# Attention scores of a quad laid side by side, and a mix back whose stationary pieces have 128 columns

## The chip, the core and the metric

The kernel runs on one core of one Trainium2 chip. The time is device time in microseconds (us) from the start to the end of one execution; the number given for the kernel is the median of its runs. Engines are named as the profile names them: PE is TensorE (a matmul moves one operand through an array that holds a stationary operand, which PEld loads), DVE is VectorE, ACT is ScalarE, POOL is GpSimd, and SP is the queue that issues the DMAs.

## What is computed

A stack of two blocks on 32 sequences of 256 tokens with 128 channels, in float32. Block 0 is a selective-scan mixer with a gated feed-forward net. Block 1 is an attention with 16 heads of 64 and 4 memory keys a head, followed by another feed-forward net. The change lies in the attention of block 1, whose core is, cut to what matters:

```python
dots = jnp.einsum('bhid,bhjd->bhij', q, k) * QK_SCALE      # j: 4 memory keys, then the tokens
dots = jnp.einsum('hg,bgij->bhij', W_pre_th, dots)         # heads mixed before the softmax
dots = jnp.where(causal[None, None], mask_value, dots)
top = jax.lax.top_k(dots, TOPK)[0]                         # TOPK = 64
dots = jnp.where(dots < top[..., -1:], mask_value, dots)
attn = jax.nn.softmax(dots, axis=-1)
attn = jnp.einsum('hg,bgij->bhij', W_post_th, attn)        # heads mixed after it: the "mix back"
out = jnp.einsum('bhij,bhjd->bhid', attn, v)
```

## The kernel before

Block 0 runs first, for all sequences (to about 860 us). Then `attention_phase` runs block 1 as a pipeline over sequences. In each period of the pipeline one sequence goes through ranking and softmax while the next one's scores are made and the one before it goes through attention, output projection and feed-forward net. Every engine has a fixed order of work, written out by hand: a period has 128 beats, and tables such as `PE_MIX`, `ACT_MIX`, `POOL_SHARE` and `DVE_SHARE` say at which beat a step stands in its engine's stream. A step then runs when its semaphores allow it; nothing is reordered at run time.

**Tiling of the scores.** 128 partitions hold 8 queries (`QG`) of 16 heads, which is one group; a sequence has 32 groups. Group `g` sees 4 + 8(g + 1) keys, and its row of scores is as wide as that of the odd group of its pair: 20, 20, 36, 36, ... 260, 260 elements. All rows of a sequence lie in one tile, `T8` (two of them, for even and odd sequences), from element `ROW[g]` on. Before the change the rows lie in the order of the groups, except that row 31 lies ahead of row 30 (`ROW`, line 1075). `side(g)` is 1 where a row lies behind that of its pair.

**Quads.** Ranking, softmax and mix back go by quads: quad i is the groups 30-2i, 31-2i, 2i, 2i+1, so two wide rows and two narrow ones, together 560 elements in every quad.

**A quad's way.** SP sends scores through DRAM to regroup them by head and query (`stage`, `regroup`; lines 1277 to 1297; one DMA a pair, but two where `side(g)` of the pair's first group is 1). PE mixes the heads of a pair (`premix`, L1371), ACT copies it to `T8` (`t_keep`, L1575), POOL adds the causal mask (`hide`, L1898). DVE finds the 64 largest of every row with rounds of eight (`rank`, `wide`, `narrow`: L1752 to L1797 for wide rows, L1719 to L1735 for narrow ones). POOL marks and drops what is below (`drop`, L1923, L1933), ACT takes the exponentials (`exps`, L1551), DVE the reciprocal of the sums (`share_out`, L1704), and POOL scales the post-mix matrix with it (`share_posts`, L1882, tile `posts`).

**The mix back** (`mix_back`, lines 1373 to 1400). It multiplies each row of scores, as stationary operand, with its `posts`, which turns it to have keys on partitions. A row is cut into pieces of at most 128 columns: `first` takes elements 0 to 127 (L1383), `second` from 128 on for the wide rows (L1387), and groups 15 and 31 have one more piece of 4 columns (L1399). A last piece has as many columns as are left of the row: 20 to 116. A quad's mix back is 6 or 7 matmuls; the profile shows two records for each matmul in float32. Results lie in two PSUM banks (`ATB`), from which ACT copies them (`at_keep`, L1588 to L1596), only as many partitions as the row has keys. `back_mixed` is raised once, by the last matmul of a quad. Attention (`attend`, L1414 to L1418) follows when all quads of a sequence are copied.

**Other lines that the prediction names.** L221, L195, L250 feed-forward matmuls; L432, L453, L1437, L1448 projections; L1356 scores (`score`, stationary operand on 64 partitions), copied by ACT at L1567; L134 spreads a layer norm's factor for DVE's last step of the norm at L140 (tiles `nc_rs` and `x_c` for the first norm, `nd_rs` and `x_d` for the second).

Of the kernel before, what the change touches and what calls it, by code (L numbers as in the profile page):

```python
# [12 lines left out]
P = 128  # L13
# [4 lines left out]
HEADS, DH, MEM, TOPK = 16, 64, 4, 64  # L18
INNER = HEADS * DH
IC = INNER // P  # L20
KEYS = MEM + SEQ
KM = HEADS * MEM
QG = P // HEADS
GROUPS = SEQ // QG
NXB = 3
QUADS = GROUPS // 4
# [6 lines left out]
HALF = GROUPS // 2  # L33
# [9 lines left out]
def seen_by(group):  # L43

    return MEM + QG * (group + 1)
# [1012 lines left out]
def attention_phase(nc, sh, ctx, out):  # L1058
# [4 lines left out]
    sems, room = sh.room, Room(nc, ctx)  # L1063
# [8 lines left out]
    def width(g):  # L1072
        return seen_by(g | 1)

    ROW = [sum(width(k) for k in range(g)) for g in range(GROUPS + 1)]
    ROW[GROUPS - 2:GROUPS] = ROW[GROUPS - 2] + KEYS, ROW[GROUPS - 2]
    T8 = room.sbs("T8_", [P, ROW[GROUPS]], 2)

    def pair_scores(b, g):
        at = min(ROW[g], ROW[g + 1])  # L1080
        return T8[b % 2][:, at:at + min(2 * width(g), 512)]

    def scores(b, g, a=0, z=None):
        z = width(g) if z is None else z
        return T8[b % 2][:, ROW[g] + a:ROW[g] + z]

    def side_by_side(b, g):

        at, w = min(ROW[g], ROW[g ^ 1]), width(g)
        return T8[b % 2][:, at:at + 2 * w].rearrange("p (two n) -> p two n", two=2)  # L1090

    def side(g):
        return int(ROW[g] > ROW[g ^ 1])

    QUAD = [(30 - 2 * i, 31 - 2 * i, 2 * i, 2 * i + 1) for i in range(QUADS)]
    PREMIX = [list(range(HALF)), [g for i in range(QUADS) for g in (30 - 2 * i, 31 - 2 * i)]]
    PAIR_AT = {g: (blk * HALF + k) // 2 for blk in range(2) for k, g in enumerate(PREMIX[blk])}

# [13 lines left out]
    NP = 8  # L1112
    posts = room.sbs("posts", [P, P], NP)
# [35 lines left out]
    TURNED = [g for g in range(GROUPS) if g not in WHOLE and g not in WIDE]  # L1149
    DROPS = [[j0 for j0 in (0, 2) if QUAD[i][j0 + 1] not in WHOLE] for i in range(QUADS)]  # L1150
    DROPS_ALL = sum(len(c) for c in DROPS)
# [7 lines left out]
    def rank_steps(i):  # L1159

        n = sum(17 for g in QUAD[i] if g in WIDE) + (QUAD[i][2] not in WIDE) + 2 * len(CUT[i])
        for g in QUAD[i]:
            if g in TURNED:
# [163 lines left out]
    def tensor(pe):  # L1327
# [45 lines left out]
        def mix_back(b, i):  # L1373

            n = GROUPS * b + 4 * i
            at0, at1 = ATB
            pe.wait_ge(posts_made, n + 4)
            if n:
                pe.wait_ge(at_kept, AT_KEEPS * b + KEPT[i])

            def first(j):
                m = min(width(QUAD[i][j]), P)
                return pe.matmul(at0[0:m, j * P:(j + 1) * P], scores(b, QUAD[i][j], 0, m), posts[(n + j) % NP][:], start=True, stop=True)  # L1383

            def second(j):
                m = min(width(QUAD[i][j]), 2 * P) - P
                return pe.matmul(at1[0:m, j * P:(j + 1) * P], scores(b, QUAD[i][j], P, P + m), posts[(n + j) % NP][:], start=True, stop=True)  # L1387

            order = [(first, 0), (first, 1)]
            if width(QUAD[i][2]) <= P // 2:  # L1390
                order += [(second, 0), (second, 1), (first, 2), (first, 3)]
            else:
                order += [(first, 2), (first, 3), (second, 0), (second, 1)]
            for one, j in order:
                last = one(j)
            for j in (1, 3):
                if QUAD[i][j] in (HALF - 1, GROUPS - 1):
                    c = P if QUAD[i][j] == HALF - 1 else 2 * P
                    last = pe.matmul(at1[0:MEM, 2 * P:3 * P], scores(b, QUAD[i][j], c, c + MEM), posts[(n + j) % NP][:], start=True, stop=True)  # L1399
            last.then_inc(back_mixed, 4)  # L1400

        def attend(b, c2):
# [48 lines left out]
        for p in range(-1, PERIODS):  # L1451
            for t in range(BEATS):
# [15 lines left out]
                for i in range(QUADS):  # L1468
                    if (b := whose(p, t, PE_MIX[i])) is not None:
                        mix_back(b, i)  # L1470
# [393 lines left out]
    def gpsimd(pool):  # L1864
        for s in sh.mixed_end:
            pool.wait_ge(s, 1)
        for b in range(2):
            pool.wait_ge(sh.mid_out[b], 16 * (SEQS // 2))
        pool.memset(T8[0][:], 0.0).then_inc(zeroed, 1)
        pool.memset(T8[1][:], 0.0)  # L1870
        pool.memset(V2[:], 0.0)
# [111 lines left out]
def program(nc, d, out):  # L1983

    with ExitStack() as ctx:
        sh = Shared(nc, ctx, d)
        with ExitStack() as inner:
            mixer_phase(nc, sh, inner)
        with ExitStack() as inner:
            attention_phase(nc, sh, inner, out)  # L1990
# [63 lines left out]
```

## Time and profile before

| | |
|---|---|
| time, median of 3 runs | 3660.3 us (3659.46 to 3661.69) |
| span of the profiled execution | 3658.1 us |
| busy, share of the span | PE 94%, DVE 93%, ACT 84%, PEld 70%, POOL 48% |
| chain that ended last | PE 64%, DVE 16%, ACT 14%, issue 3%, POOL 2%, DMA 1% |
| DMA | 210.76 MB, 58 GB/s on average |

The span is the time from the first to the last instruction of one execution. Busy shares are means over the whole span, of which the first 860 us are block 0, without any of the work that changes. The views below therefore look at stretches of block 1. In the timeline a line is a group of like instructions in a row: when the first began, how long from there to the end of the last, and in brackets the idle time of the engine before it with what ended that time. PE's matmuls overlap at their ends, so the pitch of two groups (start to start) says what a group costs, and its length is some 0.2 us more.

### The profile page before, as it was taken

How to read it: one execution, taken by the hardware profiler on the slowest of the kernel's cores; microseconds unless marked ns; L12 is line 12 of the kernel's file. 1: busy time of each engine (PE TensorE's matmuls, PEld its weight loads, DVE VectorE, ACT ScalarE, POOL GpSimd, SP SyncE). 2: the span in 40 equal slices, each digit the busy share in tenths (PEclk: the TensorE clock that was granted, in tenths of full speed). 3: DMA queues.
4: the chain of work that ended last, by engine and by line, in shares of the span. 5: the costliest groups of instructions: out<-in, count | busy, mean ns of one | idle time of the engine just before them, and what ended most of it. 6: DMA issues, size and time to landing. Idle time of an engine off the chain costs nothing.

```text
span 3658.1 us, 79012 instructions
## 1 busy us (share of the span) xinstructions
PE 3438.4 (94%) x19551; PEld 2576.4 (70%) x19551; DVE 3392.9 (93%) x18541; ACT 3074.4 (84%) x10773; POOL 1743.1 (48%) x3672
## 2 busy tenths in 40 slices
PE   5999999996899999999999999999999999999997
PEld 4888888883566666666666666666666666666665
DVE  7898888854999999999999999999999999999994
ACT  6777777856799899899999899989988899989963
POOL 0000000003666666666666566666666666666653
PEclk7999999997899999999999999999999999999998
DMA  3000000002222222222222222222222222222220
GB/s 131 13 12 12 13 12 10 11 7 73 63 74 70 70 74 78 80 71 65 65 65 66 65 65 69 73 71 74 70 75 84 65 65 65 65 66 65 64 62 4
DMA packets 254141, 210.76 MB, mean 58 GB/s; under 512 B 78000, under 2 KB 234736, under 8 KB 252912
## 3 DMA queue, kind: packets, MB, share of 16 engines
q1 hardware_dynamic: 253680, 205.70, 18.0%
q8 instruction: 156, 2.56, 0.3%
q14 instruction: 305, 2.50, 0.2%
HBM read 93.97 MB, written 111.67 MB: 56 GB/s over the span
## 4 chain that ended last, share of the span: by engine, by line
PE 64%; DVE 16%; ACT 14%; issue 3%; POOL 2%; DMA 1%; SPq 0%; DVEq 0%; ACTq 0%; POOLq 0%
PE bank L363 11%; PE bank L221 7%; DVE W L1775 5%; PE bank L1383 5%; PE bank L1371 5%; PE bank L1356 4%; DVE last L1797 3%; PE bank L331 3%; PE bank L1414 3%; PE bank L453 3%; ACT SN L1567 3%; PE bank L195 3%; PE bank L1448 3%; PE bank L1428 2%; PE bank L1387 2%
## 5 line engine op out<-in xcount | busy, mean ns | idle before, releaser
L1775 DVE MATCH_REPLACE8 W<-last,W 128x130 f32<-128x130 f32 (+18 forms) x3456 | 871.0, 259 | 0.0
L1797 DVE MAX8 last<-W 128x8 f32<-128x130 f32 (+18 forms) x3456 | 761.9, 261 | 0.0
L1882 POOL TENSOR_SCALAR posts<-post,share 128x128 f32<-128x128 f32 x1024 | 366.5, 379 | 287.2 <-DVE share L1704 278.1
L894 DVE TENSOR_TENSOR_SCAN hs<-dA,dx 128x256 f32<-128x256 f32 x512 | 348.1, 680 | 86.6 <-issue 80.2
L1551 ACT ACTIVATE T<-T,peak 128x260 f32<-128x260 f32 (+15 forms) x1024 | 410.9, 409 | 4.2 <-POOL T L1933 3.3
L1567 ACT ACTIVATE SN<-bank,rq 128x260 f32<-128x260 f32 (+1 forms) x1024 | 357.8, 424 | 61.3 <-PE bank L1356 60.1
L1371 PE MATMUL bank<-T,pre 128*128 128x40 f32 (+15 forms) x1024 | 364.8, 439 | 15.0 <-ACT T L1575 10.1
L1383 PE MATMUL bank<-posts,T 128*128 128x128 f32 (+7 forms) x2048 | 310.2, 288 | 71.5 <-POOL posts L1882 63.4
L1933 POOL TENSOR_TENSOR T<-T,below 128x520 f32<-128x520 f32 (+12 forms) x416 | 360.5, 883 | 20.1 <-DVE below L1806 4.8
L1383 PEld LDWEIGHTS bank<-posts,T 128*128 128x128 f32 (+7 forms) x2048 | 247.2, 173 | 168.6 <-POOL posts L1882 93.8
L1898 POOL TENSOR_TENSOR T<-T,w_mask 128x32 f32<-128x32 f32 x512 | 141.0, 278 | 403.5 <-ACT T L1575 401.1
L1356 PE MATMUL bank<-kT,qT 64*128 64x260 f32 (+1 forms) x2048 | 274.8, 372 | 42.8 <-ACT SN L1567 33.5
L522 POOL TENSOR_SCALAR k_sq<-k_sq 128x16 f32<-128x16 f32 x64 | 17.7, 276 | 591.9 <-DVE k_sq L535 542.3
L1923 POOL TENSOR_SCALAR below<-T,last 128x244 f32<-128x244 f32 (+3 forms) x256 | 270.2, 1055 | 33.9 <-DVE last L1795 10.6
L1371 PEld LDWEIGHTS bank<-T,pre 128*128 128x128 f32 x1024 | 168.0, 191 | 164.1 <-issue 82.8
L1775 DVE MATCH_VALUE_LOAD W<-last,W 128x8 f32 x3456 | 261.0, 76 | 0.0
L221 PE MATMUL bank<-f_b,w_f1h 128*128 128x256 f32 x1024 | 248.9, 387 | 5.7 <-ACT f_b L233 5.7
L1575 ACT ACTIVATE T<-bank 128x40 f32<-128x40 f32 (+15 forms) x512 | 208.0, 406 | 51.3 <-PE bank L1371 49.2
L1520 ACT ACT_TABLE_LOAD x192 | 246.3, 1283 | 4.5 <-POOLq L1049 1.1
L221 PE MATMUL bank<-f_a,w_f1h 128*128 128x256 f32 x1024 | 248.0, 385 | 0.0
L1356 PEld LDWEIGHTS bank<-kT,qT 64*128 64x128 f32 x2048 | 146.9, 191 | 136.1 <-ACT SN L1567 74.3
L363 PE MATMUL bank<-f_b,w_f0h 128*128 128x256 f32 x1024 | 236.5, 379 | 0.0
(244 smaller groups left out, 9584.0 us busy)
## 6 DMA issues: line engine op xcount, KB each, us to landing
scores_by_token<-SN SPq DMA_DIRECT2D x64, 520.0 KB, 2.6
scores_by_token<-SN SPq DMA_DIRECT2D x64, 396.0 KB, 3.2
scores_by_token<-SN SPq DMA_DIRECT2D x32, 780.0 KB, 3.3
scores_by_token<-SN SPq DMA_DIRECT2D x32, 264.0 KB, 2.6
scores_by_token<-SN SPq DMA_DIRECT2D x32, 260.0 KB, 2.0
T<-scores_by_token SPq DMA_DIRECT2D x32, 244.0 KB, 3.1
T<-scores_by_token SPq DMA_DIRECT2D x32, 228.0 KB, 3.3
T<-scores_by_token SPq DMA_DIRECT2D x32, 212.0 KB, 3.9
```

Of the source, the lines that this page charges most:

```text
L221: last = pe.matmul(o[:, (m % 2) * SEQ:(m % 2 + 1) * SEQ], self.w[layer][:, c, m * P:(m + 1) * P], src[:, c, :], start=c == 0, stop=c == HC ...
L363: last = pe.matmul(o[:, (m % 2) * SEQ:(m % 2 + 1) * SEQ], self.w[layer][:, c, m * P:(m + 1) * P], src[:, c, :], start=c == 0, stop=c == HC ...
L894: dve.tensor_tensor_scan(hs[j % NH][:], dA[j % ND][:], dx[b % 2][:], 0.0, ALU.mult, ALU.add).then_inc(scanned, 1)
L1356: last = pe.matmul(FRONT[(n + half) % 3][:, j * w:(j + 1) * w], qT[rows, even // 2, blk * P:(blk + 1) * P], kT[rows, even // 2, 0:w], star ...
L1371: pe.matmul(MIX[:, 0:pair.shape[-1]], pre[:], pair, start=True, stop=True).then_inc(premixed, 1)
L1383: return pe.matmul(at0[0:m, j * P:(j + 1) * P], scores(b, QUAD[i][j], 0, m), posts[(n + j) % NP][:], start=True, stop=True)
L1551: act.activation(one, one, ACT.Exp, bias=peak[k % 2][:, j:j + 1], accum_out=total[k % 4][:, j:j + 1]).then_inc(e_made, 1)
L1567: last = act.activation(SN[:, h, 0:w], FRONT[n % 3][:, j * w:(j + 1) * w], ACT.Copy, scale=rq[:, c:c + 1])
L1775: dve.match_replace(both[:, s, at:to], best[n], both[:, s, at:to], LOWEST).then_inc(ranked, 1)
L1797: dve.max(best[n], both[:, s, at:to]).then_inc(ranked, 1)
L1882: pool.tensor_scalar(posts[(4 * k + j) % NP][:], post[:], share[k % 2][:, j:j + 1], 1.0, ALU.mult, ALU.mult).then_inc(posts_made, 1)
L1933: pool.tensor_tensor(x, x, out, ALU.add).then_inc(dropped, 1)
```

## The change

Two things. First, the rows of a quad lie together in `T8`: `LAID` is the order of the groups, and `ROW` follows from it. In the quads with groups 0 to 5 the narrow rows come first and then the wide ones, in the others the wide ones come first; row 31 still lies ahead of row 30, and now row 15 lies ahead of row 14 too, so `side(14)` is 1 and the pair (14, 15) is fetched by two DMAs. `T8` is as large as before (4480 elements). Second, a piece of the mix back no longer ends with its row: `tall` takes 128 columns from the piece's start wherever the quad's 560 elements reach that far, and so reads on into the next rows of the same quad. What comes of it lands in PSUM partitions that `at_keep` doesn't read. Columns of the pieces, before and after, from the two layouts:

| quad | first, four rows, before | after | second, two rows, before | after | extra piece, before | after |
|---|---|---|---|---|---|---|
| 0 | 128 128 20 20 | 128 128 128 128 | 128 128 | 128 128 | 4 | 128 |
| 1 | 128 128 36 36 | 128 128 128 128 | 116 116 | 128 116 | | |
| 2 | 128 128 52 52 | 128 128 128 128 | 100 100 | 128 100 | | |
| 3 | 128 128 68 68 | 128 128 128 68 | 84 84 | 128 128 | | |
| 4 | 128 128 84 84 | 128 128 128 84 | 68 68 | 128 128 | | |
| 5 | 128 128 100 100 | 128 128 128 100 | 52 52 | 128 128 | | |
| 6 | 128 128 116 116 | 128 128 128 116 | 36 36 | 128 128 | | |
| 7 | 128 128 128 128 | 128 128 128 128 | 20 20 | 128 128 | 4 | 128 |

The order of a quad's matmuls is now the same for all quads; before, quads 0 to 2 had the narrow rows last. The beat tables are unchanged.

```diff
@@ -1072,9 +1072,15 @@
     def width(g):
         return seen_by(g | 1)
 
-    ROW = [sum(width(k) for k in range(g)) for g in range(GROUPS + 1)]
-    ROW[GROUPS - 2:GROUPS] = ROW[GROUPS - 2] + KEYS, ROW[GROUPS - 2]
-    T8 = room.sbs("T8_", [P, ROW[GROUPS]], 2)
+    QUAD = [(30 - 2 * i, 31 - 2 * i, 2 * i, 2 * i + 1) for i in range(QUADS)]
+    LAID = [(0, 1, 31, 30)] + [(*q[2:], *q[:2]) if q[2] < HALF // 2 - 2 else q for q in QUAD[1:-1]] + [(16, 17, 15, 14)]
+    LAID = [g for four in LAID for g in four]
+    ROW = [sum(width(k) for k in LAID[:LAID.index(g)]) for g in range(GROUPS)]
+    T8 = room.sbs("T8_", [P, sum(width(g) for g in range(GROUPS))], 2)
+
+    def quad_end(i):
+
+        return max(ROW[g] + width(g) for g in QUAD[i])
 
     def pair_scores(b, g):
         at = min(ROW[g], ROW[g + 1])
@@ -1092,7 +1098,6 @@
     def side(g):
         return int(ROW[g] > ROW[g ^ 1])
 
-    QUAD = [(30 - 2 * i, 31 - 2 * i, 2 * i, 2 * i + 1) for i in range(QUADS)]
     PREMIX = [list(range(HALF)), [g for i in range(QUADS) for g in (30 - 2 * i, 31 - 2 * i)]]
     PAIR_AT = {g: (blk * HALF + k) // 2 for blk in range(2) for k, g in enumerate(PREMIX[blk])}
 
@@ -1378,25 +1383,25 @@
             if n:
                 pe.wait_ge(at_kept, AT_KEEPS * b + KEPT[i])
 
+            def tall(j, c):
+                m = min(quad_end(i) - ROW[QUAD[i][j]] - c, P)
+                return scores(b, QUAD[i][j], c, c + m), m
+
             def first(j):
-                m = min(width(QUAD[i][j]), P)
-                return pe.matmul(at0[0:m, j * P:(j + 1) * P], scores(b, QUAD[i][j], 0, m), posts[(n + j) % NP][:], start=True, stop=True)
+                x, m = tall(j, 0)
+                return pe.matmul(at0[0:m, j * P:(j + 1) * P], x, posts[(n + j) % NP][:], start=True, stop=True)
 
             def second(j):
-                m = min(width(QUAD[i][j]), 2 * P) - P
-                return pe.matmul(at1[0:m, j * P:(j + 1) * P], scores(b, QUAD[i][j], P, P + m), posts[(n + j) % NP][:], start=True, stop=True)
-
-            order = [(first, 0), (first, 1)]
-            if width(QUAD[i][2]) <= P // 2:
-                order += [(second, 0), (second, 1), (first, 2), (first, 3)]
-            else:
-                order += [(first, 2), (first, 3), (second, 0), (second, 1)]
-            for one, j in order:
+                x, m = tall(j, P)
+                return pe.matmul(at1[0:m, j * P:(j + 1) * P], x, posts[(n + j) % NP][:], start=True, stop=True)
+
+            for one, j in ((first, 0), (first, 1), (first, 2), (first, 3), (second, 0), (second, 1)):
                 last = one(j)
             for j in (1, 3):
                 if QUAD[i][j] in (HALF - 1, GROUPS - 1):
                     c = P if QUAD[i][j] == HALF - 1 else 2 * P
-                    last = pe.matmul(at1[0:MEM, 2 * P:3 * P], scores(b, QUAD[i][j], c, c + MEM), posts[(n + j) % NP][:], start=True, stop=True)
+                    x, m = tall(j, c)
+                    last = pe.matmul(at1[0:m, 2 * P:3 * P], x, posts[(n + j) % NP][:], start=True, stop=True)
             last.then_inc(back_mixed, 4)
 
         def attend(b, c2):
```

## Rows read from the trace of the kernel before

**Rows 1.** the page: span, and busy time of each engine

```profile
span 3658.1 us, 79012 instructions
...
PE 3438.4 (94%) x19551; PEld 2576.4 (70%) x19551; DVE 3392.9 (93%) x18541; ACT 3074.4 (84%) x10773; POOL 1743.1 (48%) x3672
```

**Rows 2.** stretches: busy (x) of PE, PEld, DVE, ACT, POOL; PEclk, DMA, GB/s

```profile
2396.50:2399.90 3.40, 3.39 (x13) 2.73 (x14) 3.40 (x32) 2.23 (x8) 1.99 (x6) 0.51 0.52 210
1800.00:1884.76 84.76, 81.36 (x502) 58.36 (x500) 84.11 (x533) 76.84 (x301) 53.62 (x115) 1.00 0.23 70
```

**Rows 3.** waits of DVE, 1000 to 3500 us: total, times, longest

```profile
DVE W L1752 <- POOL T L1898: 10.3, 29, 0.4
...
DVE x_d L140 <- PE bank L134: 3.2, 3, 1.1
...
DVE share L1704 <- ACT T L1551: 1.1, 3, 0.4
...
DVE x_c L140 <- PE bank L134: 0.6, 1, 0.6
```

**Rows 4.** timeline, DVE and POOL at the start of quad 0's ranking

```profile
1810.98 0.47 DVE L1795 MAX8 last<-W 128x8 f32<-128x124 f32 x2
...
1811.62 0.25 POOL L1898 TENSOR_TENSOR T<-T,w_mask 128x32 f32<-128x32 f32 x1
...
1811.91 0.43 DVE L1752 TENSOR_TENSOR W<-T 128x260 f32<-128x260 f32 x1 [0.36 <-POOL T L1898]
```

**Rows 5.** timeline, PE: mix backs of quads 3 and 1, with what follows

```profile
1800.46 1.04 PE L1383 MATMUL bank<-posts,T 128*128 128x128 f32 x8
1801.34 0.60 PE L1387 MATMUL bank<-posts,T 128*84 128x128 f32 x4
1801.78 0.56 PE L1371 MATMUL bank<-T,pre 128*128 128x232 f32 x2
...
1861.18 1.89 PE L221 MATMUL bank<-f_a,w_f1h 128*128 128x256 f32 x8
1862.91 1.03 PE L221 MATMUL bank<-f_b,w_f1h 128*128 128x256 f32 x4
...
1865.82 0.71 PE L1383 MATMUL bank<-posts,T 128*128 128x128 f32 x4
1866.37 0.60 PE L1387 MATMUL bank<-posts,T 128*116 128x128 f32 x4
1866.90 0.63 PE L1383 MATMUL bank<-posts,T 128*36 128x128 f32 x4
1867.46 1.99 PE L221 MATMUL bank<-f_b,w_f1h 128*128 128x256 f32 x8
1869.29 0.31 PE L1371 MATMUL bank<-T,pre 128*128 128x40 f32 x2
```

**Rows 6.** timeline, SP: regrouping a first half, and the next DMA

```profile
1863.42 3.94 SPq L1297 DMA_DIRECT2D T<-scores_by_token  x8
1873.71 0.34 SPq L1278 DMA_DIRECT2D scores_by_token<-SN  x1
```

**Rows 7.** timeline, PE and then DVE, where the granted clock was low

```profile
2396.51 1.20 PE L1356 MATMUL bank<-kT,qT 64*128 64x260 f32 x4 [0.65 <-ACT SN L1567]
...
2402.50 0.42 DVE L140 TENSOR_TENSOR x_d<-n_cen,bank 128x256 f32<-128x256 f32 x1 [1.08 <-PE bank L134]
```

**Rows 8.** timeline, DVE: the start of quad 0's ranking, three periods in a row

```profile
2324.29 0.43 DVE L1752 TENSOR_TENSOR W<-T 128x260 f32<-128x260 f32 x1 [0.36 <-POOL T L1898]
...
2410.22 0.43 DVE L1752 TENSOR_TENSOR W<-T 128x260 f32<-128x260 f32 x1 [0.37 <-POOL T L1898]
...
2495.38 0.43 DVE L1752 TENSOR_TENSOR W<-T 128x260 f32<-128x260 f32 x1 [0.36 <-POOL T L1898]
```

**Rows 9.** timeline, PE: the last quad of the last sequence

```profile
3610.58 1.04 PE L1387 MATMUL bank<-posts,T 128*20 128x128 f32 x4
...
3613.11 0.65 PE L1414 MATMUL bank<-AT,V 128*64 128x256 f32 x4 [1.15 <-ACT AT L1596]
```

## What the change was predicted to do

> **What bounds the kernel now.** I read the page first, then the busy time of a stretch inside block 1, then the waits of the engine that is fullest there, and last the timeline around the mix backs and around each of these waits.
>
> The page gives PE 94% and DVE 93% of the span [rows 1], and its chain names PE most often, so PE looks like the bound. The stretch of one period says otherwise: of 84.76 us DVE is busy 84.11, PE 81.36, ACT 76.84, POOL 53.62 [rows 2]. PE has 3.40 us a period in which it does nothing, DVE 0.65. Where two engines are this full, the chain runs over either of them; the question is who waits for whom. In 2500 us DVE waits 10.3 us for POOL's masks at L1752, 3.2 and 0.6 us for PE at L140, and 1.1 us for ACT's exponentials [rows 3]: 15.2 us together, 0.6%. Only 3.8 us of that, in four places, wait for PE. So block 1 is bound by DVE's rankings, and a faster PE can bring no more than what DVE waits.
>
> The 10.3 us are 29 waits of 0.36, one a period, at the start of quad 0's ranking. Does PE stand behind them? DVE's last two MAX8 of the quad before it start at 1810.98 and end at 1811.45; POOL's mask starts at 1811.62, lasts 0.25, and DVE goes on at 1811.91 [rows 4]. In POOL's stream the wait of `drop` for these MAX8 (L1916) stands ahead of that mask. It is a hand-over from DVE to POOL and back, and PE has no part in it: it keeps its 0.36 however early the premix comes.
>
> **Part 1, the switches between narrow and full pieces.** The pitch of groups (start to start) in quad 3, where no piece has 64 columns or fewer: 0.88 for eight records, 0.44 for four, 1.32 for all twelve, whether a piece has 128, 84 or 68 columns [rows 5]. Quad 1, with two rows of 36 columns: from the group of 116 columns to that of 36 it is 0.53 in place of 0.44, so 0.09 for going in. The four narrow records take 0.56 in place of 0.44, so 0.12. After them eight records of L221 take 1.83 where the same group takes 1.73 between 1861.18 and 1862.91, so 0.10 for coming out [rows 5]. Narrow pieces are not shorter (0.14 a record against 0.11), and an excursion into them costs 0.09 + 0.12 + 0.10 = 0.31 us. Quads 0, 2, 5, 6 and 7 have one excursion each as well, six a sequence with quad 1's. In quad 2 the step out stays, since what follows (L1356, on 64 partitions) is another arrangement of the array anyway: 6 x 0.31 - 0.10 = 1.76 us a sequence. The change widens all these pieces to 100 columns or more, and all of it goes.
>
> **Part 2, wider loads.** 24 matmuls of a sequence, three a quad, get wider stationary pieces: 1744 columns more by the table of the change, each loaded twice. Rows 5 show four records at 0.44 both with 84 columns and, as half of the 0.88 group, with 128 and 68; the digits would hide 0.01 at most. 24 matmuls are 12 groups of four: at most 0.12 us. I take 0.06, and 1.76 - 0.06 = 1.7 us a sequence, or 54 us of PE time over 32 sequences. A rule speaks against the change here: the Trainium skill, "TensorE: Matmul & The Clock Gate", section "LDWEIGHTS (loading the stationary operand)", says that a load takes its number of columns divided by 1.2, in ns. By it the loads grow by an estimated 1744 x 2 / 1.2 = 2.9 us a sequence, which is more than the switches give back, if they were exposed. The rows show them hidden under the matmul before, as long as the arrangement doesn't change; and even exposed they would take 1.2 us net out of PE's idle 3.4, so that the time of the kernel would be the same by either.
>
> **Where the 1.7 us go.** They don't reach DVE. PE's idle time grows from 3.40 to some 5.1 us a period, mostly ahead of the mix backs that wait for `posts` and of the score matmuls that wait for ACT's copies. ACT gets `back_mixed` earlier and waits less at L1588. Neither shortens DVE's 84.11 us, nor the hand-over.
>
> **Part 3, the order.** In quads 0 to 2 `second` now runs ahead of the narrow rows. ACT is released by the last matmul alone, so this moves nothing: 0. No wait is added: the mix back already waits for `posts` of all four rows, which come after all four exponentials, so the neighbouring rows that `tall` reads are finished.
>
> **Part 4, the new layout.** DVE, ACT and POOL do the same instructions on the same widths at other addresses, all multiples of 4 elements as before: 0. The pair (14, 15) takes two DMAs on SP. Eight of them take 3.94 us to issue, 0.49 each; SP's next DMA comes 6.4 us after the eighth is out (1873.71 against 1867.36) [rows 6]. What waits for the landing of this pair and the one before it is the premix of 232 elements, at 1801.78 in one period [rows 5] and so at 1886.5 in the next, 18.7 us after the new DMA would be issued. Hidden; without that cover it would cost 0.5 us a period, and in the first sequence, where the pipeline fills, it might show once: 0 to 0.5, I take 0.
>
> **Part 5, the end.** After the last ranking the rest is a chain of PE, ACT and POOL, and the last mix back lies on it: attention waits for ACT's copies of it [rows 9]. Going into its narrow piece falls away, 0.09 at full clock; here the record lengths are longer (1.04 for the four against 0.60 to 0.63), so perhaps 0.2. Going out stays, since attention uses 64 columns. I take -0.1.
>
> **The sum.** 3658.1 for the span, -0.1 at the end, 0 elsewhere: 3658.0. The median of the runs is 3660.3, 2.2 above the profiled span; so 3660.2 us. What a measurement of this kernel can tell from no change is about 0.2%, 7.3 us.
>
> **Rival 1, PE's clock (slower).** From 2396.50 to 2399.90 the granted clock was 0.51, the lower of the two levels, 1.2 in place of 2.4 GHz [rows 2]. Just before it PE had been waiting 0.65 us for ACT's copy, amid score matmuls and pieces of a single column. PE came late with the spread at L134, and DVE waited 1.08 us at L140 [rows 7]. From one start of quad 0's ranking to the next it took 85.93 us there and 85.16 in the next, against 84.76: 1.6 us for one such drop [rows 8]. Three waits of 3.2 us in all say that it was so in three periods of some 30 [rows 3]. The change makes PE idle more, just ahead of the scores (quads 0 and 1) and of quad 7's `posts` (quads 5 and 6). If the clock then drops in ten periods in place of three, 7 x 1.6 = 11.2 us are added: 3671. It decides from five more on (7.3 / 1.6). For it: these stretches are the emptiest already. Against it: PE also gets there earlier, which shortens the very wait at L140, and ACT moves up with it. By the Trainium skill, the same page, "Part 1: The HAM clock gate", the low clock is the default and activity releases it, so that more idling means more of it; the trace agrees in that the drop followed a stretch with waits, and whether 1.7 us more are enough no row tells.
>
> **Rival 2, PE binds after all (faster).** If DVE's waits all hang on PE in a way that the waits view puts down to others, the 15.2 us in 2500 go: 16.4 us over the 2700 of block 1, so 3644. Rows 4 speak against it, and DVE's 84.11 us of 84.76 stay.
>
> **Rival 3, the switches stay.** If the pitch hangs on something else than the number of columns, mix backs are as long as before, and the time too: 3660. Quads 3 and 4, without switches at 84 and 68 columns, speak against it.
>
> **Chances.** Forecast 0.65; rival 1 0.22; rival 2 0.06; rival 3 0.05; that the drops of the clock vanish, for -5 us, 0.02. Faster is rival 2 and a little of the unknown, 0.08; slower is rival 1, 0.22; within 0.2% is the rest, 0.70. The range goes up to rival 1's time and a little over, 3672, and down to 3654, which takes in the vanished drops and the ends of parts 2, 4 and 5. The forecast's own range is 3656 to 3664.
>
> **What the profile after would show.** Quad 1's mix back and quad 7's with all groups at 0.11 a record, and no record of L1383, L1387 or L1399 with 64 columns or fewer (part 1). PE's busy time in a period down by 1 to 2 us and its waits up by as much, at L1383 for `posts` above all. ACT's wait at L1588 smaller. DVE's 0.36 at L1752 still there, the period still 84.7 to 84.8. Nine DMA issues in the first half's regrouping, with no premix waiting for them. The count of DVE's waits at L140 decides rival 1. I am wrong if DVE's busy time or its hand-over changes, that is, if the period does.

## The result, and the profile after

The changed kernel takes 3685.2 us (median of 4 runs, 3681.9 to 3688.4), the kernel before, measured beside it, 3659.9 us (4 runs): a ratio of 1.0072, 95% interval 1.0058 to 1.0086. It is slower, by 26 us and outside the range, which ended at 3672. Lines have moved: L1383, L1387 and L1399 are now L1392, L1396 and L1404, L1356 is L1361, L1371 is L1376, L1575 is L1580, L1752 and L1755 are L1757 and L1760, L1882 is L1887, L1898 is L1903, L1925 and L1933 are L1930 and L1938.

The page first (as [rows 1]) and one undisturbed period, from one start of quad 0's ranking to the next (as the second of [rows 2]):

```profile
span 3684.6 us, 79044 instructions
...
PE 3421.0 (93%) x19551; PEld 2603.2 (71%) x19551; DVE 3416.4 (93%) x18541; ACT 3073.3 (83%) x10773; POOL 1753.3 (48%) x3672
```

```profile
1394.52:1480.02 85.50, 80.47 (x503) 58.82 (x502) 84.88 (x533) 76.76 (x300) 54.27 (x114) 1.00 0.22 69
```

PE's time went down and DVE's went up, with the same 533 instructions: 84.88 us against 84.11. The period is 85.50 in place of 84.76. And what DVE waits for has hardly changed (as [rows 3]; waits of DVE, 1000 to 3500 us):

```profile
DVE W L1757 <- POOL T L1903: 9.9, 29, 0.4
DVE x_c L140 <- PE bank L134: 3.7, 6, 0.6
DVE share L1709 <- ACT T L1556: 0.4, 2, 0.2
```

So the time sits inside DVE's instructions, where no view of waits looks. I compared a period of each kernel instruction by instruction. Two are longer in 21 of the 30 periods, all undisturbed ones among them: the first two steps (maximum and minimum of a row's halves, two inputs) for the pair (14, 15) at the start of quad 7's ranking. The timeline there, DVE and POOL, first before and then after:

```profile
1458.28 0.25 POOL L1898 TENSOR_TENSOR T<-T,w_mask 128x32 f32<-128x32 f32 x1 [0.96 <-ACT T L1575]
...
1458.63 1.47 POOL L1925 TENSOR_SCALAR below<-neg,last 128x116 f32<-128x116 f32 x2
...
1459.76 0.27 DVE L1752 TENSOR_TENSOR W<-T 128x132 f32<-128x132 f32 x1
1459.95 0.28 DVE L1755 TENSOR_TENSOR W<-T 128x132 f32<-128x132 f32 x1
...
1460.18 1.51 POOL L1933 TENSOR_TENSOR T<-T,below 128x328 f32<-128x328 f32 x2
```

```profile
1464.12 1.50 POOL L1930 TENSOR_SCALAR below<-neg,last 128x116 f32<-128x116 f32 x2
...
1465.71 1.57 POOL L1938 TENSOR_TENSOR T<-T,below 128x328 f32<-128x328 f32 x2
...
1466.06 0.69 DVE L1757 TENSOR_TENSOR W<-T 128x132 f32<-128x132 f32 x1
1466.66 0.77 DVE L1760 TENSOR_TENSOR W<-T 128x132 f32<-128x132 f32 x1
```

POOL's two additions (328 and 232 elements; they drop what `drop` has marked in quad 6) used to start 0.42 us behind DVE's first step, and now start 0.35 us ahead of it. Then each step of DVE ends 0.16 us after the addition beside it: the additions run 1465.71 to 1466.58 and 1466.55 to 1467.27, the steps end at 1466.74 and 1467.43, 0.69 and 0.77 us long in place of 0.27 and 0.28. From the first step to what follows both it is 1.29 us (the next instruction starts at 1467.35), where it was 0.40 (1460.16): 0.89 more. DVE arrives 0.12 earlier, since a marking of its own just ahead, no longer beside POOL's mask, takes 0.54 in place of 0.62. The period as a whole is 0.74 longer, x30 = 22 us.

In five other periods, each with a fall of PE's clock (a short stretch at the lower granted clock, of which more below), POOL's first addition starts 0.03 us behind DVE's first step. That step keeps its 0.27; the addition takes 0.98 in place of 0.88, and it is the second step that waits for its end:

```profile
1124.26 0.27 DVE L1757 TENSOR_TENSOR W<-T 128x132 f32<-128x132 f32 x1
1124.29 1.68 POOL L1938 TENSOR_TENSOR T<-T,below 128x328 f32<-128x328 f32 x2
1124.45 0.97 DVE L1760 TENSOR_TENSOR W<-T 128x132 f32<-128x132 f32 x1
```

Why POOL comes earlier is one row of ACT, its copy of the pair of 168 elements, first before, then after:

```profile
1457.88 0.32 ACT L1575 ACTIVATE T<-bank 128x168 f32<-128x168 f32 x1
```

```profile
1463.38 0.32 ACT L1580 ACTIVATE T<-bank 128x168 f32<-128x168 f32 x1
```

Counted from the start of quad 0's ranking (1388.10 and 1394.52) that is 69.78 and 68.86. POOL's mask of this pair had been waiting for the copy (0.96 in the rows before); its marks and additions stand behind the mask in its stream, and came along, from 72.08 to 71.19. DVE's step stayed, at 71.66 and 71.54.

The other 4 us of the profiled difference (26.5): the first start of quad 0's ranking is 2.7 later, which is scatter, since over the fourteen profiles of this case it lies anywhere from 876.4 to 882.2 us, behind code that none of them changes; 2.2 lie behind the last start of quad 0's ranking, the last collision among them; and what the 30 periods take beyond the undisturbed length (falls of the clock, mostly) sums up to 10.0 before and 9.4 after.

### The profile page after: what moved, and what is told of

Same layout as the page of the kernel before. It is cut to its first block, busy times and chain, and to the rows that moved or that the text cites. A ratio compares the mean times of both kernels' runs of the same rounds, so it can differ in the third digit from the quotient of the medians.

```text
span 3684.6 us, 79044 instructions
## 1 busy us (share of the span) xinstructions
PE 3421.0 (93%) x19551; PEld 2603.2 (71%) x19551; DVE 3416.4 (93%) x18541; ACT 3073.3 (83%) x10773; POOL 1753.3 (48%) x3672
## 4 chain that ended last, share of the span: by engine, by line
PE 53%; DVE 33%; POOL 5%; ACT 5%; issue 3%; DMA 1%; SPq 0%; DVEq 0%; ACTq 0%; POOLq 0%
PE bank L363 11%; DVE W L1780 11%; DVE last L1802 7%; PE bank L221 4%; DVE W L1732 3%; PE bank L1419 3%; PE bank L453 3%; PE bank L331 3%; PE bank L1376 3%; PE bank L1433 3%; PE bank L1453 3%; PE bank L195 2%; PE bank L1392 2%; PE bank L1361 2%; POOL posts L1887 2%
## 5 line engine op out<-in xcount | busy, mean ns | idle before, releaser
L1887 POOL TENSOR_SCALAR posts<-post,share 128x128 f32<-128x128 f32 x1024 | 366.5, 376 | 371.9 <-DVE share L1709 364.4
L1392 PEld LDWEIGHTS bank<-posts,T 128*128 128x128 f32 (+4 forms) x2048 | 258.9, 194 | 195.3 <-POOL posts L1887 170.5
L1392 PE MATMUL bank<-posts,T 128*128 128x128 f32 (+4 forms) x2048 | 297.4, 290 | 104.8 <-POOL posts L1887 102.4
L1376 PE MATMUL bank<-T,pre 128*128 128x40 f32 (+15 forms) x1024 | 365.7, 439 | 16.1 <-ACT T L1580 11.1
L1938 POOL TENSOR_TENSOR T<-T,below 128x520 f32<-128x520 f32 (+12 forms) x416 | 367.1, 898 | 20.2 <-DVE below L1811 5.0
L1361 PE MATMUL bank<-kT,qT 64*128 64x260 f32 (+1 forms) x2048 | 276.3, 374 | 42.2 <-ACT SN L1572 34.3
L522 POOL TENSOR_SCALAR k_sq<-k_sq 128x16 f32<-128x16 f32 x64 | 17.6, 275 | 595.5 <-DVE k_sq L535 542.3
L1903 POOL TENSOR_TENSOR T<-T,w_mask 128x32 f32<-128x32 f32 x512 | 143.4, 285 | 327.1 <-ACT T L1580 324.1
L1376 PEld LDWEIGHTS bank<-T,pre 128*128 128x128 f32 x1024 | 168.5, 193 | 170.2 <-issue 84.4
L221 PE MATMUL bank<-f_b,w_f1h 128*128 128x256 f32 x1024 | 245.8, 384 | 5.4 <-ACT f_b L233 5.4
L221 PE MATMUL bank<-f_a,w_f1h 128*128 128x256 f32 x1024 | 244.6, 382 | 0.0
L1361 PEld LDWEIGHTS bank<-kT,qT 64*128 64x128 f32 x2048 | 147.0, 191 | 133.9 <-ACT SN L1572 95.1
L1580 ACT ACTIVATE T<-bank 128x40 f32<-128x40 f32 (+15 forms) x512 | 206.6, 404 | 41.2 <-PE bank L1376 39.8
```

The source lines that it names most:

```text
L221: last = pe.matmul(o[:, (m % 2) * SEQ:(m % 2 + 1) * SEQ], self.w[layer][:, c, m * P:(m + 1) * P], src[:, c, :], start=c == 0, stop=c == HC ...
L1361: last = pe.matmul(FRONT[(n + half) % 3][:, j * w:(j + 1) * w], qT[rows, even // 2, blk * P:(blk + 1) * P], kT[rows, even // 2, 0:w], star ...
L1376: pe.matmul(MIX[:, 0:pair.shape[-1]], pre[:], pair, start=True, stop=True).then_inc(premixed, 1)
L1392: return pe.matmul(at0[0:m, j * P:(j + 1) * P], x, posts[(n + j) % NP][:], start=True, stop=True)
L1887: pool.tensor_scalar(posts[(4 * k + j) % NP][:], post[:], share[k % 2][:, j:j + 1], 1.0, ALU.mult, ALU.mult).then_inc(posts_made, 1)
L1938: pool.tensor_tensor(x, x, out, ALU.add).then_inc(dropped, 1)
```

## The experiments

Each ratio is to the kernel before on the same chip, with its 95% interval. The period is the median of 30, the lower of the two in the middle; an undisturbed one of before is 84.76. "Steps" are DVE's two steps of the pair (14, 15), "lead" is how far POOL's first addition starts ahead of the first step, and "falls" counts stretches from 965 to 3500 us where the granted clock fell below full. The step lengths, lead and falls are from the one profiled execution.

| kernel | ratio | period | steps | lead | falls |
|---|---|---|---|---|---|
| before | 1 | 84.79 | 0.27 0.28 | -0.42 | 4 |
| after | 1.0072 (1.0058 to 1.0086) | 85.50 | 0.69 0.77 | +0.35 | 11 |
| e1_layout_only | 1.0002 (0.9993 to 1.0012) | 84.75 | 0.27 0.28 | -0.42 | 3 |
| e2_pe_padded | 1.0077 (1.0062 to 1.0092) | 85.70 | 0.27 0.28 | -1.24 | 5 |
| e3_before_hide_late | 1.0089 (1.0073 to 1.0104) | 85.71 | see below | +1.25 | 7 |
| e4_pool_delay | 1.0030 (1.0018 to 1.0042) | 85.35 | 0.27 0.28 | -0.42 | 19 |
| e6_before_clip | 0.9983 (0.9973 to 0.9993) | 84.69 | 0.27 0.28 | -0.42 | 3 |
| e8_wide_567 | 1.0024 (1.0014 to 1.0033) | 84.76 | 0.27 0.28 | -0.33 | 13 |
| e9_wide_012 | 1.0083 (1.0068 to 1.0098) | 85.80 | 0.69 or 0.84, 0.77 | +0.35 or +0.20 | 7 |
| e10_one_input | 1.0021 (1.0012 to 1.0031) | 85.33 | 0.27 0.46 | +0.35 | 18 |
| e11_fill_567 | 1.0004 (0.9995 to 1.0014) | 84.75 | 0.27 0.28 | -0.34 | 6 |
| e12_fill_567_clip | 0.9975 (0.9964 to 0.9986) | 84.42 | 0.27 0.28 | -0.34 | 2 |
| e13_after_fill | 1.0057 (1.0040 to 1.0074) | 85.57 | 0.68 0.77 | +0.35 | 1 |
| e14_after_fill_delay | 1.0010 (1.0001 to 1.0019) | 84.99 | 0.27 0.28 | -0.42 | 11 |

The theory: POOL's additions meet DVE's steps. The rivals: the new layout or its additional DMA costs the time, or PE's clock does.

### The layout alone

The change with its new `ROW`, but the old pieces in the old order:

```diff
-            def tall(j, c):
-                m = min(quad_end(i) - ROW[QUAD[i][j]] - c, P)
...
+                m = min(width(QUAD[i][j]), P)
+                return pe.matmul(at0[0:m, j * P:(j + 1) * P], scores(b, QUAD[i][j], 0, m), ...)
```

> The new order of the rows in T8 (with two DMAs for the pair 14, 15), but the mix back cut into the same pieces and in the same order as before. Theory (the collision): PE, no longer waiting at the switches, lets ACT's copies and POOL's mask come 0.9 us earlier, so that POOL's two additions in the drop of quad 6 run at the same time as DVE's four max and min steps at the start of quad 7's ranking, and two of these take 0.69 and 0.77 us in place of 0.27 and 0.28; with the old pieces PE is slow again, the period is 84.76 us and the time 3660, within 0.2% of before. Rival (the layout): DVE reads the pair 14, 15 slower where it lies now; then the period is 85.5 and the time 3683 to 3686.

3659.5 us, 1.0002. The layout and its ninth DMA are innocent. What is left of the change is its pieces and their order in quads 0 to 2.

### PE as slow as before

After, with two matmuls into a dead place behind the mix back of every quad with an excursion:

```diff
+            if i not in (3, 4):
+                x, m = tall(1, P)
+                for n_ in (P, 48):
+                    last = pe.matmul(at1[0:m, P:P + n_], x, posts[(n + 1) % NP][:, 0:n_], start=True, stop=True)
             last.then_inc(back_mixed, 4)
```

> The changed kernel, with 128-column pieces, but in the six quads that had narrow pieces the last wide piece is multiplied once more, and once more with 48 columns moving, some 0.30 us a quad, about what a switch to narrow pieces and back took. The values are the same. Theory (the collision): only PE's time matters, so the max and min steps of the pair 14, 15 take 0.27 and 0.28 us again, the period is 84.8 and the time 3658 to 3666. Rival (the layout or the wide pieces themselves): 85.5 and 3683 to 3688.

A miss: 3686.9 us, though the collision is gone (0.27 and 0.28, POOL 1.24 late). The padding overshot: it takes 0.35 to 0.38 us in five of the six quads, up to the start of what follows, where 0.30 was meant, and the period has 82.21 us of PE's time against 81.36 before. POOL's mask is now held back to 1465.68, 71.56 behind the start of quad 0's ranking, and PE and ACT with it. DVE now waits for them (1000 to 3500 us):

```profile
DVE share L1713 <- ACT T L1560: 18.5, 29, 0.6
DVE W L1761 <- POOL T L1907: 11.2, 29, 0.5
DVE x_d L140 <- PE bank L134: 8.7, 5, 1.8
```

It doesn't speak to the collision, and it corrects me in something else: with 0.85 us more of PE's time, DVE waits for ACT's exponentials in every period, and the chain that ended last is PE 74%, ACT 16% and DVE 5%. That "block 1 is bound by DVE's rankings" was true by less than a microsecond.

### The collision in the kernel before

The kernel before, with nothing of the change: only POOL's mask of that pair moved behind `drop` of quad 6, so that nothing holds the marks and additions back.

```diff
-    POOL_PREMIX = [[92, 94, 95, 97, 112, 117, 120, 128], ...
+    POOL_PREMIX = [[92, 94, 95, 97, 116, 117, 120, 128], ...
```

> The kernel before, with one entry of POOL's order changed: the mask of the fifth pair of a sequence's first half goes behind the drop of quad 6 in place of ahead of it, so that the drop no longer waits for ACT's copy of that pair. PE, ACT and DVE have the order, pieces and layout of before. Theory (the collision): the drop's marks start 0.9 to 1.1 us earlier, its additions meet DVE's max and min steps, these take 0.4 us longer twice or more, and the time is 3678 to 3692. Rival (layout, or PE's clock): POOL's order has nothing to do with it, 3660.

3692.2 us, 1.0089, with PE and the layout untouched. DVE and POOL in its timeline:

```profile
1468.50 1.58 POOL L1933 TENSOR_TENSOR T<-T,below 128x328 f32<-128x328 f32 x2 [0.18 <-DVE below L1806]
1468.56 0.99 DVE L1755 TENSOR_TENSOR W<-T 128x148 f32<-128x148 f32 x1
...
1469.76 0.48 DVE L1752 TENSOR_TENSOR W<-T 128x132 f32<-128x132 f32 x1
...
1470.16 0.34 DVE L1755 TENSOR_TENSOR W<-T 128x132 f32<-128x132 f32 x1
```

POOL is so early here that it meets another step as well: L1755 takes 0.99 where its like takes 0.30. The three are 0.69 + 0.21 + 0.06 = 0.96 us a period longer, and the period is 85.71, 0.95 longer than an undisturbed one of before. The meeting is enough by itself to cost this much.

### The collision taken out of the changed kernel

After, with two idle POOL instructions, 0.9 us together, ahead of `drop` of quad 6:

```diff
+            if i == 6:
+                for n, w in enumerate((512, 16)):
+                    pool.wait_ge(idled, 2 * b + n + 1)
+                    pool.tensor_scalar(idle[:, 0:w], idle[:, 0:w], 1.0, 1.0, ALU.mult, ALU.mult).then_inc(idled, 1)
```

> The changed kernel, with two idle POOL instructions (0.9 us together) ahead of the drop of quad 6, on a tile that nobody reads. PE stays as fast as in the changed kernel. Theory (the collision): the additions come after DVE's max and min steps, as before, the period is 84.8, and the time 3658 to 3668; what is left over before is what PE's clock costs. Rival (the layout, or PE's clock): 3683 to 3688, or more.

3671.0 us, above the 3668 that I had expected at most: it gives 15 of the 26 us back. The steps are short again and the undisturbed period is 84.72. What is left goes with the last column of the table: 19 falls of the clock, and with them a median period of 85.35. Most of these belong to this kernel, though, and not to the changed one. Six stand 7 to 8 us behind the start of quad 0's ranking, as in the changed kernel (more on them under "Which quads do it"). Thirteen stand 71 to 72 us behind it, and there DVE waits 0.2 us for PE's spread (`x_d`) and 0.3 for ACT's exponentials, 13 times each; the changed kernel has five falls at that place, and in three of the five the period stays at 85.49.

Then POOL's additions in quad 6 as instructions of one input:

```diff
+                if i == 6:
+                    pool.tensor_scalar(x, x, 1.0, 1.0, ALU.mult, ALU.mult).then_inc(dropped, 1)
+                    continue
                 pool.tensor_tensor(x, x, out, ALU.add).then_inc(dropped, 1)
```

> The changed kernel, but POOL's two additions in the drop of quad 6 (two inputs each) are replaced by an instruction of one input on the same elements, which writes them back unchanged; so keys below the 64th stay in quad 6, and nothing else is left out. Theory (two instructions of two inputs, one on DVE and one on POOL, shut each other out): POOL works over the same stretch, yet DVE's steps at L1757 and L1760 take 0.27 and 0.28 us, and the time is 3658 to 3670. Rival (any POOL instruction at that moment slows DVE): the steps stay at 0.5 us or more, 3675 or more.

3668.2 us, DVE and POOL:

```profile
1458.90 0.86 POOL L1939 TENSOR_SCALAR T<-T 128x328 f32<-128x328 f32 x2
...
1459.25 0.27 DVE L1757 TENSOR_TENSOR W<-T 128x132 f32<-128x132 f32 x1
1459.44 0.46 DVE L1760 TENSOR_TENSOR W<-T 128x132 f32<-128x132 f32 x1
```

I had expected one input to set the steps free. It doesn't: the second still ends 0.14 us after POOL's second instruction (0.46 in place of 0.28, in 24 of 30 periods). The collision shrank because POOL's instructions are half as long, 0.47 and 0.43 against 0.88 and 0.72. Its 18 falls of the clock all stand 71 to 72 us behind the start of quad 0's ranking, so its time tells no more than that.

### Which quads do it

`tall` only in quads 3 to 7, or only in quads 0 to 4 (the others as before):

```diff
-                m = min(quad_end(i) - ROW[QUAD[i][j]] - c, P)
+                end = quad_end(i) if i in wide_ones else ROW[QUAD[i][j]] + width(QUAD[i][j])
+                m = min(end - ROW[QUAD[i][j]] - c, P)
```

> The changed kernel, with quads 0 to 2 cut and ordered as before (narrow pieces last) and 128-column pieces in quads 3 to 7. Theory (the collision): the time that moves ACT's copy of the fifth pair and so POOL's drop of quad 6 is what PE saves in quads 0 to 2, which stand 11 to 31 us ahead of it in a period; what it saves in quads 5 to 7 is taken up by waits for posts and for ACT's copies of V in between. So POOL's addition comes 0.3 to 0.5 us after DVE's step, as before, the steps take 0.27 and 0.28 us, and the time is 3654 to 3666. Rival (all of PE's time counts alike, wherever it is saved): half of the shift stays, the steps take 0.4 us or more, 3670 or more.

> The other half: 128-column pieces in quads 0 to 4, quads 5 to 7 cut as before. Theory (the collision): POOL's addition comes 0.2 to 0.4 us before DVE's step, both steps take 0.6 to 0.8 us, the period is 85.5, the time 3678 to 3690. Rival (all of PE's time counts alike): 3665 to 3675, between before and after.

The second has the collision in full (0.69 and 0.77 in about half of the periods, 0.84 and 0.77 in most others; 1.0083, or 3690.6 us, just above what I expected); the first has not (0.27 and 0.28, period 84.76). So it is the excursions saved in quads 0 to 2 that bring ACT's copy forward. But the first is at 1.0024, above what I expected of it: 13 periods are longer, 86.08 against 84.76. PE and PEclk there, first the timeline and then two stretches of windows (columns as [rows 2]):

```profile
1227.77 1.66 PE L1395 MATMUL bank<-posts,T 128*128 128x128 f32 x8 [1.87 <-POOL posts L1893]
...
1313.85 1.16 PE L1395 MATMUL bank<-posts,T 128*128 128x128 f32 x8 [1.55 <-POOL posts L1893]
```

```profile
1226.00:1228.00 2.00, 0.23 (x2) 0.23 (x3) 2.00 (x15) 2.00 (x9) 1.87 (x6) 1.00 0.03 8
1228.00:1230.00 2.00, 2.00 (x12) 2.00 (x12) 2.00 (x11) 2.00 (x11) 0.97 (x4) 0.57 0.00 0
```

In one period PE waits 1.87 us for quad 7's `posts` and then works at a granted clock of 0.57, close to the lower level of 1.2 GHz; in the next it waits 1.55, and the eight records take 1.16 as at 2.4 GHz. The wait alone doesn't decide: before the change it is 1.5 to 1.6, after it 2.0 in nearly all periods, as PE saves time ahead of it, and there the clock falls in some periods only. The cost of a fall is two things of about the same size. The products that POOL takes of PE's late results (L1955) come late as well and meet a step of DVE's, and later on DVE waits for PE's spread. DVE's waits, 1000 to 3500 us, and the timeline of the step, in this period and in the next:

```profile
DVE x_c L140 <- PE bank L134: 8.1, 13, 0.6
```

```profile
1238.18 2.52 POOL L1955 TENSOR_TENSOR gate<-gate,f_a 128x512 f32<-128x512 f32 x2
...
1239.98 0.97 DVE L1763 TENSOR_TENSOR W<-T 128x228 f32<-128x228 f32 x1
...
1323.04 2.52 POOL L1955 TENSOR_TENSOR gate<-gate,f_a 128x512 f32<-128x512 f32 x2
...
1326.07 0.40 DVE L1763 TENSOR_TENSOR W<-T 128x228 f32<-128x228 f32 x1
```

The products end at 1240.70 in the one, past the step's start, and at 1325.56 in the other, ahead of it. 0.64 for the wait and 0.97 in place of 0.40 for the step give 1.21 of the 1.32. There are 13 waits and 13 long steps, 12 of them with 0.94 to 0.97.

### The clock taken out

Idle matmuls ahead of quad 7's wait for `posts`, five in e8's kernel and six in the changed one; and the last also with e4's delay on POOL:

```diff
+            if i == QUADS - 1:
+                pe.wait_ge(at_kept, AT_KEEPS * b + KEPT[i])
+                for _ in range(5):
+                    pe.matmul(at0[:, 0:P], sh.ident[:], sh.ident[:], start=True, stop=True)
             pe.wait_ge(posts_made, n + 4)
```

> The kernel with 128-column pieces in quads 3 to 7 only, and in addition five idle matmuls (the identity by itself, 1.1 us together) on PE ahead of its wait for the posts of quad 7, into a PSUM bank that is overwritten next. Theory (the second term is PE's clock): what PE saves in quads 5 to 7 becomes idle time at this wait, the granted clock drops behind it in 13 periods, each 1.3 us longer with DVE waiting 0.64 us at L140; with the idle time filled the drops go there, at most 4 periods have one, and the time is 3656 to 3663. Rival (the 0.64 us come from PE being late for another reason): more matmuls make PE later still, 3669 or more.

> The changed kernel, with six idle matmuls (1.3 us) on PE at the same wait. Theory (collision and clock are two terms): the collision stays, since ACT and POOL are as early as before, 22 us; the drops of the clock behind the wait for quad 7's posts go. The time is 3677 to 3684, with the steps of the pair 14, 15 at 0.69 and 0.77 us. If the collision were a matter of the clock, they would be 0.27.

> The changed kernel with both: the six idle matmuls, and the 0.9 us of idle POOL instructions ahead of the drop of quad 6 that gave 3671. Theory (both terms gone): 3658 to 3666. If the 12 us that stayed there came from the idle POOL instructions themselves, which make the second norm's root late, it stays at 3668 or more.

Filling takes e8 from 1.0024 to 1.0004, 7 us. All 13 falls of e8 stood behind quad 7's `posts`, about 7 us behind the start of quad 0's ranking; none does now, the 6 that are left (4 had been expected at most) stand 72 us behind it, and DVE's waits for `x_c` are gone. It takes the changed kernel from 1.0072 to 1.0057, some 5 us, though these two intervals overlap (and 3675.7 is just below the 3677 to 3684 expected). In the profiles it is clearer: of the changed kernel's 11 falls the six behind quad 7's `posts` are gone, and so are DVE's six waits for `x_c`; one fall is left, 71 us behind the start, and the collision is in place (0.68 and 0.77, period 85.57). Fill and delay together give 1.0010. So the collision alone is worth 1.0057 against 1.0010, 17 us, and more without the delay's own cost: 11 falls 71 to 72 us behind the start, as in e4, with periods of 85.35 against 84.70, and DVE waits of 3.1 us for ACT's exponentials and 2.4 for `x_d`, where the filled kernel has 0.2 and none. 17 + 5.5 is about the 22 of the trace.

### What the hand-over was, and a better kernel

In the kernel before, POOL's squared-key step at L522 (`POOL_K_CLIP`) moved behind quad 0's mask, and then the same in e11's kernel:

```diff
-    POOL_K_CLIP = (2, 23)
+    POOL_K_CLIP = (3, 23)
```

> The kernel before, with the clip of the key norms on POOL (L522) one beat later, behind the mask of quad 0's pair. It stands between POOL's posts and that mask, for which DVE waits 0.36 us every period. If that wait is a matter of POOL's order, it goes, and the time is 3648 to 3655. If DVE has another wait right behind (the norm's spread from PE, 0.1 us of slack), or the mask waits for ACT's copy anyway, it is 3656 to 3664.

> The same, and the clip of the key norms on POOL one beat later, behind the mask of quad 0's pair, which took 6 us off the kernel before. If both hold, 3645 to 3656, and at or below the 3653.6 of the clip alone where PE's 0.8 us a period in quads 5 to 7 are of use to DVE's waits at L140; if they are of none, 3652 to 3658.

3653.6 us, 0.9983: the 10.3 us that DVE waited for this mask [rows 3] are 1.0, in 3 places. Part of it comes back elsewhere (DVE's waits in the kernel with the move alone, 1000 to 3500 us):

```profile
DVE share L1704 <- ACT T L1551: 5.5, 26, 0.4
DVE x_d L140 <- PE bank L134: 3.0, 3, 1.0
DVE W L1752 <- POOL T L1898: 1.0, 3, 0.4
```

The kernel with wide pieces in quads 3 to 7, the filling and the move takes 3646.4 us against 3656.8 of the kernel before beside it, 0.9975 (0.9964 to 0.9986), period 84.42. It is faster than before and than e11, the same without the move. Whether it beats the move alone (0.9983, 0.9973 to 0.9993) the two intervals leave open; the profiles say so, with an undisturbed period of 84.42 against some 84.7 and nearly no waits of DVE left:

```profile
DVE x_d L140 <- PE bank L134: 0.7, 1, 0.7
DVE share L1719 <- ACT T L1566: 0.5, 2, 0.3
DVE W L1767 <- POOL T L1913: 0.4, 1, 0.4
```

## Why the prediction was wrong, by its steps

**The step that failed is "Where the 1.7 us go"**: "They don't reach DVE. ... Neither shortens DVE's 84.11 us, nor the hand-over." I had ACT moving up and stopped there. Behind ACT stood POOL, which waits 0.96 us for the copy, and behind its mask stood the additions, 0.42 us away from a step of DVE's that can't run beside them. I asked only who waits less, and took DVE's busy time for a constant. Its instructions have no fixed length: two of them grew by 0.42 and 0.49, and the 84.11 us became 84.88. I had a side for this in the text ("I am wrong if DVE's busy time ... changes"), but no rival and no price. The Trainium skill, "SBUF — State Buffer", section "🔬 SBUF: two separate sides", states it: a DVE instruction with two SBUF inputs and a GpSimd instruction that reads SBUF share a pair of ports, which the first to start holds for its whole length. The traces agree for the additions and the one-input instructions of e10 (the step ends 0.14 to 0.17 us after POOL's instruction in e3, e10 and after), and for the products (0.25 in e8). They agree the other way round too: POOL's mask, 0.25 us by itself, takes 0.51 where it starts just behind a step of DVE's and ends 0.11 behind it (the kernel before):

```profile
1567.94 0.41 DVE L1755 TENSOR_TENSOR W<-T 128x244 f32<-128x244 f32 x1
1567.95 0.51 POOL L1898 TENSOR_TENSOR T<-T,w_mask 128x32 f32<-128x32 f32 x1 [2.44 <-ACT T L1575]
```

They don't quite for POOL's marks. The 128x116 pair that starts at 1458.63 lies beside DVE steps of 0.30 and 0.27, unslowed although the marks started first. There it is POOL that pays: its mark of 128x132 elements takes 0.73 us alone and 1.23 where it runs beside the two steps of 260 elements (0.43 and 0.42, where those of 244 elements take 0.40). Only in the five periods with POOL's addition 0.03 us late does a step beside a mark take 0.38 in place of 0.30. What sets the marks apart is open.

**Part 1 was right.** No mix back has a piece of 64 columns or fewer. Quad 1 and what follows it, after:

```profile
1447.87 1.16 PE L1392 MATMUL bank<-posts,T 128*128 128x128 f32 x8
1448.87 0.60 PE L1396 MATMUL bank<-posts,T 128*128 128x128 f32 x4
1449.31 1.89 PE L221 MATMUL bank<-f_b,w_f1h 128*128 128x256 f32 x8
1451.04 0.31 PE L1376 MATMUL bank<-T,pre 128*128 128x40 f32 x2
```

From the mix back's start to L1376 it is 3.17 us, against 3.47 in [rows 5]: 0.30 for 0.31 forecast, and L221 is back at 1.73. **Part 2 too**: four records still take 0.44. PE as a whole saves less than was forecast: in the undisturbed period it is busy 80.47 us against 81.36, 0.9 less, and over the whole run 17 us less (3421.0 against 3438.4), where 1.7 a sequence and 54 in all had been the forecast. The difference is not explained. As forecast, its idle time went ahead of `posts` (from 46.9 to 83.1 us between 1000 and 3500 us).

**Part 4 holds:** e1 gives 1.0002 for the layout and its DMA. **Part 3**, the order in quads 0 to 2, no run separates from the pieces. **Part 5** can't be read under a scatter of several us.

**[Rows 4] were misread.** The mask comes at the end of POOL's own work, not of a hand-over from DVE: `drop`'s wait stands behind it. POOL before it, in the kernel before:

```profile
1386.65 0.72 POOL L1882 TENSOR_SCALAR posts<-post,share 128x128 f32<-128x128 f32 x2
...
1387.45 0.28 POOL L522 TENSOR_SCALAR k_sq<-k_sq 128x16 f32<-128x16 f32 x1
...
1387.81 0.25 POOL L1898 TENSOR_TENSOR T<-T,w_mask 128x32 f32<-128x32 f32 x1
```

It waits for nothing there; it is behind with its list, and moving L522 away took the wait off, which "it keeps its 0.36" excludes. The conclusion that PE has no part in it still held (29 waits, 9.9 us, after).

**Rival 1 had the mechanism, not the size.** The clock did fall more often, 11 times against 4. Six of the 11 stand where it was said, behind the wait for quad 7's `posts`, and their periods are 1.2 to 1.7 us longer, in part once more by a meeting of DVE and POOL (in five of the six, L1757 of 228 elements takes 0.88 to 0.94 in place of 0.40). The other five stand 71 to 73 us behind the start of quad 0's ranking; three of their periods are 85.49, so that they cost nothing there. Before, one fall stood at the first place (1.6 us) and three at the second, where DVE had to wait 1.1 us for `x_d` and each cost 1.6 us over two periods. The periods with falls of either kind come to some 8 us beyond the undisturbed length after, and to some 6 before; with all else that disturbs a period the two are level, 9.4 and 10.0. So by the traces the clock is about 2 of the 26 us, though filling the gap takes some 5 us off the changed kernel (e13). Rival 2 falls (PE is busy 0.9 us a period less and DVE's waits didn't shrink), rival 3 too.

## What to carry to other kernels

When an engine off the critical path becomes faster, follow the chain of those that it releases up to the next shared resource, also where nobody on it is critical: here PE, ACT, POOL, and then a stretch in which two steps of DVE's can't run beside POOL's additions. In a kernel whose schedule repeats, look in the timeline for near misses between a POOL instruction and a DVE instruction of two inputs; 0.4 us of distance, once in each of some 30 periods, was worth 22 us. Compare the busy time of the bounding engine at an equal count of instructions before looking at waits, as such a loss stands in no wait.

## What the runs showed of the hardware that I had not expected

- A DVE step of two inputs that starts while an addition or product of POOL's runs ends 0.15 to 0.25 us after that instruction ends (or takes its own length, where that is longer): 0.27 became 0.69, 0.28 became 0.77, 0.30 became 0.99, and 0.40 became 0.97.
- Five idle matmuls a sequence, 320 records of PE in all, into a gap in which PE was waiting anyway, took 7 us off (1.0024 to 1.0004): none of the 13 falls of the granted clock behind the gap was left.
- A single POOL instruction of 0.28 us on 16 elements, ahead of a mask in the stream, was worth 6 us of 3660.
